# A recurrence of 512 steps on VectorE: copies, normaliser logarithms and output adds given to ScalarE and GpSimd, and the side work dealt over the eight steps anew

## The reference

```python
def step(state, inp):                       # state: (batch, head, 16, 16)
    r_t, k_t, v_t, w_t, a_t, kk_t = inp
    sa = jnp.einsum('bhij,bhj->bhi', state, -kk_t)
    state = w_t[..., None] * state + sa[..., None] * (kk_t * a_t)[:, :, None, :] + k_t[..., None] * v_t[:, :, None, :]
    norm = jnp.sqrt(jnp.mean(state * state, axis=-1, keepdims=True))
    state = state / (norm + EPS_STATE)
    o_t = jnp.sum(state * r_t[..., None], axis=-1)
    return (state, o_t)
...
out = g * out @ Wo.T
nrm = jnp.sqrt(jnp.mean(out * out, axis=-1, keepdims=True))
out = x_g + out / (nrm + EPS_RMS) * ln_weight      # x_g = x + 0.1 * convolution(x)
```

## Time and profile before

| | us |
|---|---|
| median of 3 runs (lowest, highest) | 2437.0 (2434.69, 2437.7) |
| the profiled execution's own time | 2441.28 |
| its span | 2439.2 |
| DVE busy | 2187.4 (90%) |
| PE busy | 1925.3 (79%) |
| ACT busy | 1585.6 (65%) |
| POOL busy | 903.2 (37%) |

### The profile page before, as it was taken

How to read it: one execution, slowest core, us unless ns; L and a number is a source line. 1 busy time by engine, 2 the same in 40 slices (tenths; PEclk the granted TensorE clock), 3 DMA queues, 4 the chain that set the end, 5 groups by cost and what they waited for, 6 DMA issues and landing times.

```text
span 2439.2 us, 47897 instructions
## 1 busy us (share of the span) xinstructions
PE 1925.3 (79%) x12321; PEld 1556.6 (64%) x12321; DVE 2187.4 (90%) x8800; ACT 1585.6 (65%) x5168; POOL 903.2 (37%) x1528
## 2 busy tenths in 40 slices
PE   5888888788888878888888878688887877344787
PEld 3555555455687867777777767677777767343555
DVE  6888887689619999999999999999999999999887
ACT  4878888577646665666666666666666565444776
POOL 0000000011105555555555555555555555555110
PEclk8999999699977787787877777987778777655899
DMA  5000000000000000000000000000000000000011
GB/s 183 17 17 22 17 21 23 3 1 1 1 1 1 1 1 1 1 1 1 1 1 1 1 1 1 1 1 1 1 1 1 1 1 1 1 1 1 1 35 35
DMA packets 14353, 25.02 MB, mean 10 GB/s; under 512 B 1280, under 2 KB 12032, under 8 KB 13824
## 3 DMA queue, kind: packets, MB, share of 16 engines
q1 hardware_dynamic: 14080, 21.97, 3.0%
HBM read 12.27 MB, written 4.19 MB: 7 GB/s over the span
## 4 chain that ended last, share of the span: by engine, by line
DVE 57%; issue 16%; PE 15%; ACT 6%; POOL 0%; DVEq 0%; POOLq 0%; ACTq 0%
DVE pn L1563 11%; DVE bank L1579 10%; DVE U L1620 8%; DVE xs L1551 5%; DVE bank L1568 5%; DVE kv L1612 4%; PE bank L282 3%; PE bank L267 2%; ACT prob L923 2%; PE bank L585 2%; DVE bank L1609 1%; PE bank L761 1%; DVE bank L1588 1%; DVE bank L1532 1%; PE bank L632 1%
## 5 line engine op out<-in xcount | busy, mean ns | idle before, releaser
L1748 POOL TENSOR_TENSOR wu<-U,stg 128x256 f32<-128x256 f32 x512 | 318.6, 622 | 682.2 <-DVE U L1620 682.2
L750 PE MATMUL bank<-U,ident 128*128 128x128 f32 x2048 | 464.2, 399 | 81.6 <-ACT go L1064 69.3
L750 PEld LDWEIGHTS bank<-U,ident 128*128 128x128 f32 x2048 | 426.7, 238 | 121.5 <-issue 90.6
L761 PE MATMUL bank<-stack,tm 128*128 128x64 f32 x1792 | 336.4, 374 | 145.7 <-ACT tm L994 137.2
L1213 ACT ACTIVATE xs<-U 128x128 f32<-128x128 f32 x1024 | 261.5, 302 | 275.5 <-DVE U L1620 271.6
L761 PEld LDWEIGHTS bank<-stack,tm 128*128 128x128 f32 x1792 | 325.6, 284 | 162.9 <-ACT tm L994 153.0
L1563 DVE TENSOR_REDUCE pn<-xs 128x16 f32<-128x256 f32 x1024 | 377.6, 408 | 0.6 <-issue 0.2
L1701 POOL TENSOR_TENSOR kv<-stg 128x256 f32<-128x256 f32 x513 | 318.7, 621 | 0.0
L1131 ACT ACTIVATE small<-pn 128x16 f32<-128x16 f32 x513 | 110.9, 216 | 295.0 <-DVE pn L1563 295.0
L735 PE MATMUL bank<-wcat,yT 128*128 128x224 f32 x1024 | 294.6, 447 | 2.5 <-issue 2.0
L1579 DVE TENSOR_TENSOR bank<-wu,bank 128x128 f32<-128x128 f32 x1024 | 292.0, 285 | 1.1 <-POOL wu L1748 0.8
(11 more groups left out here) (214 smaller groups left out, 3567.6 us busy)
## 6 DMA issues: line engine op xcount, KB each, us to landing
out_x<-x SPq DMA_DIRECT2D x8, 512.0 KB, 2.9
x<-in_x SPq DMA_DIRECT2D x1, 3584.0 KB, 17.7
Vs<-V SPq DMA_DIRECT2D x8, 384.0 KB, 4.6
...
```

The source lines that it names most:

```text
L750: last = pe.matmul(rsum.rearrange("p (t i) -> p t i", i=HD), ident[:, :], steps[:, :, :, j], start=(j == 0), stop=(j == HD - 1))
L761: last = pe.matmul(bank[3 + g][:, e * CH:(e + 1) * CH], tm[:, g * (PB // 2) + e, :, :].rearrange("p a c -> p (a c)"), stack[:, :], start=T ...
L1748: pool.tensor_tensor(ij(wu[:, :]), ij(U[:, half if j else 1 - half, (j - 1) % STEPS, :]), col(stg[:, half, j, TW, :]), ALU.mult).then_inc( ...
```

## The change

From DVE it takes the copies of kk and kk*a, the copies to `hist`, L1506, L1523 and L1528.

- The rows kk and kk*a are copied into bank 0 by ACT, in two operations for each half round (`copy_kk`, `copy_kka`), behind the squares of j = 2 and 6, and of j = 1 and 5. kk is taken from R directly; the slot for it in `stg`, and `stage_kk`, are gone. kk*a has two buffers, kk has one.
- ACT takes the logarithm straight from `sring`, twice a round (behind the squares of j = 0 and j = 4), 64 values each; `hist` is gone.
- These three wait for both L1551 of the next step (`beside_sums`), so that they run while DVE sums.
- A tile of the convolution, and of the output with its scale, is copied by ACT to `otmp` (`evacuate_convolution` in j = 5, `scale_outputs` in j = 7, both ahead of the squares). POOL multiplies the output by the weight and adds both to x.
- ACT's other side work moves: `evacuate_outputs` from behind the squares of j = 7 to ahead of those of j = 0, `factors` from j = 2 to ahead of those of j = 3, the second exponential of the decay and the small functions of the output's norm to ahead of those of j = 5, the gates' logarithm from j = 4 to j = 7.
- DVE waits for the copies of kk and kk*a at the first step of each half round, and once in each of jj = 1, 2 and 3, for the logarithm, for kk*a and for kk, before L1568.

The core of the diff (its waits on PE, which follow the new counts, and its semaphores' names are left out):

```diff
         zz = bank[0][:, 0:HD * HD]
-        kkz = bank[0][:, 256:384].rearrange("p (t q j) -> p t q j", q=2, j=HD)
-        sring = bank[0][:, 384:448].rearrange("p (t i) -> p t i", i=HD)
+        kkr = bank[0][:, 256:320].rearrange("p (t j) -> p t j", j=HD)
+        kkar = bank[0][:, 320:448].rearrange("p (g t j) -> p g t j", g=2, j=HD)
+        sring = bank[0][:, 448:512].rearrange("p (t i) -> p t i", i=HD)
...
+                act.activation(otmp, bank[6][:, 0:D], ACT.Copy).then_inc(C["x1"], 1)
...
+                act.activation(otmp, bank[6][:, 0:D], ACT.Copy, scale=oss[:, 2, 0:1]).then_inc(O["t"], 1)
+
+            def copy_kk(row):
+
+                act.activation(kkr, R[:, bass.ds(row, RENORM), QKK * HD:(QKK + 1) * HD], ACT.Copy).then_inc(S["kk"], 1)
+
+            def copy_kka(half, g):
+
+                act.activation(kkar[:, g, :, :], stg[:, half, g * RENORM:(g + 1) * RENORM, TKKA, :],
+                               ACT.Copy).then_inc(S["ka"], 1)
...
-                act.wait_ge(S["h"], last)
-                act.wait_ge(G["f2"], k)
-                act.activation(ls[:, :, :], hist[:, half, :, :], ACT.Ln).then_inc(G["ls"], 1)
+            def log_norms(g):
+
+                act.activation(ls[:, g * RENORM:(g + 1) * RENORM, :], sring, ACT.Ln).then_inc(G["ls"], 1)
+
+            def beside_sums(t1):
+
+                for e in range(2):
+                    act.wait_ge(T[e]["x"], t1)
...
                             if j == 0:
+                                if m >= 1:
+                                    evacuate_outputs(n, m - 1)
+                                elif n >= 1:
+                                    evacuate_outputs(n - 1, NB - 1)
                                 normalise(n, m)
...
                             if j == 3:
+                                factors(it, 1 - half)
                                 evacuate_features(n, m)
...
                             if j == 5:
+                                retention(1, it + 1, row_next)
                                 output_rms(n, m, 0)
+                                output_rms(n, m, 1)
+                                evacuate_convolution(n, m)
...
                             if j == 7:
                                 evacuate_pairs(n, m, 1)
+                                scale_outputs(n, m)
                             for e in range(2):
-                                act.wait_ge(T[e]["u"], t0 + (j + 1))
+                                act.wait_ge(T[e]["u"], t1)
                                 act.activation(xs[:, e, 1, :], rows8(U[:, half, j, :], e), ACT.Square).then_inc(T[e]["sq"], 1)
...
-                            if j == 7:
-                                evacuate_outputs(n, m)
+                            if t1 < L and (j + 1) % RENORM == 1:
+                                beside_sums(t1 + 1)
+                                act.wait_ge(S["sg"], t1)
+                                act.wait_ge(G["f2"], it + (j + 1) // RENORM)
+                                log_norms(0 if j + 1 > RENORM else 1)
+                            if t1 < L and (j + 1) % RENORM == 2:
+                                beside_sums(t1 + 1)
+                                if t1 > RENORM:
+                                    for e in range(2):
+                                        act.wait_ge(T[e]["z"], t1 - 2)
+                                act.wait_ge(G["ka"], it + 1 + g)
+                                copy_kka(half if g == 0 else 1 - half, 1 - g)
+                            if t1 < L and (j + 1) % RENORM == 3:
+                                beside_sums(t1 + 1)
+                                copy_kk(row_it + RENORM if g == 0 else row_next)
...
                             if jj == 0:
                                 dve.wait_ge(S["kk"], it * 2 + (g + 1))
+                                dve.wait_ge(S["ka"], it * 2 + (g + 1))
...
-                            if jj == 1:
-
-                                dve.wait_ge(S["sg"], t0 + j)
-                                if g == 0:
-                                    dve.tensor_copy(hist[:, 1 - half, RENORM:, :], sring).then_inc(S["h"], 1)
-                                else:
-                                    dve.tensor_copy(hist[:, half, 0:RENORM, :], sring).then_inc(S["h"], 1)
...
+                            if jj == 1:
+                                dve.wait_ge(G["ls"], it * 2 + (g + 1))
+                            if jj == 2:
+                                dve.wait_ge(S["ka"], it * 2 + (g + 2))
+                            if jj == 3:
+                                dve.wait_ge(S["kk"], it * 2 + (g + 2))
...
                             if j == 6:
-                                add_convolution(n, m)
                                 add_output(n, m, 0)
-                            if j == 7:
-                                add_output(n, m, 2)
...
                                 dve.reciprocal(lam, sring[:, jj - 1, :]).then_inc(S["lam"], 1)
-                                if g == 0:
-                                    kk_rows(half, 1)
-                                else:
-                                    dve.wait_ge(G["kk"], it + 2)
-                                    dve.wait_ge(G["ka"], it + 2)
-                                    kk_rows(1 - half, 0)
-                                if j == 7:
-                                    add_output(n, m, 3)
                                 dve.wait_ge(S["lam"], it * 2 + (g + 1))
...
+            def add_convolution(n, m):
...
+                pool.tensor_tensor(xt, xt, otmp, ALU.add).then_inc(C["x1"], 1)
...
+                pool.tensor_tensor(otmp, otmp, ln_w[:, :], ALU.mult).then_inc(O["t"], 1)
...
+                pool.tensor_tensor(xt, xt, otmp, ALU.add).then_inc(O["x"], 1)
```

158 lines of the change are left out of this document (86 added, 72 removed).

## The result

| | before | after |
|---|---|---|
| median of the runs, us | 2436.3 (2434.69 to 2437.7) | **2401.98** (2399.8 to 2405.28) |
| runs | 4 | 4 |
| ratio, with its 95% interval | 1 | 0.9861 (0.9843 to 0.9878) |
| profiled execution, us (span) | 2441.28 (2439.2) | 2399.92 (2398.1) |
| start of the recurrence, first to last product, rest | 724.95, 1528.6, 185.7 | 717.28, 1495.9, 184.9 |

The change makes the kernel faster by 34.3 us (1.4%); 2396.3 was predicted, within 2385 to 2412. The recurrence (from the first to the last L1572, in before L1551) is 32.7 us shorter. The other 8.4 of the profiled difference lie ahead of it (7.7) and behind it (0.7). In the twelve profiled executions of this study, whose code ahead of the recurrence is nearly the same, it starts anywhere from 713.3 us to 725.0 us, so I give that part no cause.

The account below looks back on a forecast made before the run. The recurrence was taken as bound by DVE, which was full while ACT was not. The terms 15.4 + 8.0 + 12.1 + 9.0 - 3.8 = 40.7 came off 2437.0, giving 2396.3 us, with an 8-in-10 range of 2385 to 2412.

Parts of the forecast that it names:

- output, 24 rounds: Step 7 of chunks 3, 5 and 7: removing L1523 and L1528 from DVE saves 0.64 each round, 15.4 us.
- convolution, 32 rounds: Step 6 in 32 rounds: removing L1506 from DVE saves 0.25 each, 8.0 us, as it partly covers a wait.
- `hist` copies: Steps 1 and 5: removing two copies a round saves 12.1 of 17.9 us, the rest covering waits for ACT's squares.
- kk copies: Rescaling steps: removing the copy saves 0.07, not 0.18, as L1609 waits for the reciprocal; 128 times, 9.0 us.
- more waits: First product of each half round: a third semaphore costs 0.03, 128 times, -3.8 us; ends 0 and -5.1.
- ACT late: Steps 0 and 5: ACT's operations ahead of the squares just fit, taken as 0; bound -10.8 us.
- POOL: POOL's 80 added operations fit its idle time, at most one a step: 0, unless `wu` is late.
- Rival 1: Steps 0 and 5: ACT's operations ahead of the squares don't fit; costs 10.8, giving 2407.1, or 2418 at twice that; chance 0.20.
- Rival 2: Step 5's wait for squares goes too, up to 5.8 more, and waits cost nothing, 3.8 more: 2387; chance 0.09.
- Rival 3: ACT's operations behind the squares delay the root by 0.1 in 384 steps: 38 us back, 2435; chance 0.04.
- Rival 4: DVE is held while POOL runs the 80 rounds' `otmp` adds and products: 49.6 us, 2445.9, slower; chance 0.05.
- Rival 5: DVE waits at the new semaphores as long as the removed operations took: 2413.6 at best, 2437 at worst; chance 0.03.

Follow-up runs that it names:

- experiment 2: Changed kernel without the two repeated copy waits at each half round's first product, row-sum wait moved to step 0's second multiplication: 2399.34 us, ratio 0.9838.
- experiment 3: Changed kernel with the `hist` copies back on DVE and ACT's logarithm reading `hist` again: 2413.72 us, one run.
- experiment 4: Changed kernel with the 64-value kk copy back on DVE between reciprocal and rescaling, kk*a staying on ACT: 2406.19 us, one run.
- experiment 1: Changed kernel with ACT's evacuation of the row sums moved from ahead of step 4's squares to behind them: 2397.86 us, ratio 0.9830.
- experiment 7: Changed kernel with the edits of experiment 1 and experiment 2, and wait orders swapped for root, sums and new state: 2350.57 us, ratio 0.9644.
- experiment 9: Changed kernel with `evacuate_outputs` back behind step 7's squares, now behind the gates' logarithm: 2399.33 us, one run.
- experiment 8: Changed kernel with two more 128x256 POOL operations per round, results unused: 2399.95 us, one run.

## Why the prediction came out as it did

**The recurrence** was to be shorter by 36 to 46 us, or the forecast was wrong by its own words. It is shorter by 32.7, or 36.0 by the medians of the steps, and the rest of the program moved as well, by 8.4 in the profiled executions. The time lies in the range, 5.7 us above the forecast; the sum was too high, and the range was wide enough. By terms:

| term | predicted | measured |
|---|---|---|
| output, 24 rounds | 15.4 | 15.4 (24 x (0.664 - 0.024)) |
| convolution, 32 rounds | 8.0 | 7.8 |
| `hist` copies | 12.1 | 10.8 (8.3 in step 1, 2.5 in step 5) |
| kk copies | 9.0 | 5.4 |
| more waits | -3.8 | -3.6 |
| ACT late | 0 (bound -10.8) | -0.5 (step 1 of chunks 2 and 4) |
| POOL | 0 | 0 |
| late squares of step 2 gone | not foreseen | 1.5 (24 x 0.064) |
| steps beyond their medians | not foreseen | -3.4 |

For kk and the waits the table of steps gives only their difference. Steps 3 and 7 won 0.027 and 0.024, times 64 (3.3), and steps 0 and 4 lost 1.5, which leaves 1.8. With the 3.6 of the waits (experiment 2) the copies come to 5.4. The late squares of step 2 are the 0.12 of experiment 3. The last term is what the medians don't hold; the column adds to 33.4, where 32.7 is the length measured, since the last step of all lies outside it.

**The term that was mis-sized** is that of the copies of kk: "So L1609 can come to 1130.42 from 1130.49: 0.07, not 0.18", times 128, 9.0. Its first half held: L1616 starts 0.29 behind the reciprocal, where 0.28 was forecast, and experiment 4 shows that this wait and not the copy sets it. What failed is that the 0.07 was carried to the end of the step unseen. Behind L1616's start the next product follows after 1362.40 - 1361.57 = 0.83 now, and after 1131.28 - 1130.49 = 0.79 in the earlier trace rows. Of these 0.04 the waits of the product are 0.016. The rest lies in L1616 itself: its two halves start 0.208 apart in the records instead of 0.192, and its mean is longer. The group in before and in after:

```profile
L1609 DVE TENSOR_TENSOR bank<-bank,small 128x128 f32<-128x128 f32 x254 | 60.8, 284 | 0.0
```

```profile
L1616 DVE TENSOR_TENSOR bank<-bank,small 128x128 f32<-128x128 f32 x256 | 63.7, 294 | 4.4
```

Why it is 10 ns longer is not shown. A copy of 64 values ahead of it (experiment 4) leaves its halves 0.208 apart too.

**The `hist` copies** went nearly as forecast step by step: 0.13 in step 1 (0.14), 0.036 in step 5 (0.05), nothing in chunks 1 and 6, all in chunk 7. The wait for the squares in step 5 was read rightly, and experiments 1 and 3 show it from both sides. Its size, 0.41 from the square's start to the sums, is 0.31 of squaring and 0.10 of hand-over, of which 0.06 was the order of the sums' own two waits (experiment 7). In chunk 1 the sums still come late, as in the earlier trace rows: 968.54 - 967.93 = 0.61.

```profile
967.93 0.47 DVE L1572 TENSOR_TENSOR xs<-U,bank 128x128 f32<-128x128 f32 x2
968.54 0.74 DVE L1577 TENSOR_REDUCE pn<-xs 128x16 f32<-128x256 f32 x2
```

**Rival 1** (ACT late in more steps) happened in the smallest form: step 1 of chunks 2 and 4 has its sums 0.412 behind the product and takes 2.830, 16 x 0.028 = 0.5 us. The margin of 0.1 that I had worked out from neighbours held in all other places and failed in these two. It was smaller than the 0.12 by which an evacuation can start later (see the last section).

**Rival 2** (more is won) didn't, but its parts were there to be had: the wait in step 5 gives 5.6 by the order of ACT (experiment 1), and the waits of the product 3.6 (experiment 2).

**Rival 3** (the root late) didn't, but experiment 9 shows it where one operation on ACT stands 0.12 later. What failed beside it is the premise that "this stretch is DVE's, and only what shortens DVE's chain shortens it". What I had missed is that the root was late all along, by the order of its own two waits. I had read the earlier trace rows (293.9 us idle, released by DVE) as ACT waiting for DVE, which is so, and concluded that DVE sets the pace, which isn't: 0.06 of each step was the hand-over itself. The forecast survived it because it went by differences between steps, not by busy time: output, `hist` and kk were ahead of the sums or behind the normaliser, where the same chain of DVE and ACT runs through DVE, and L1506, which stood beside the root, was counted with the 0.25 that it cost.

**Rival 4** (POOL takes what DVE gives) is excluded: the sums above leave nothing for it, and experiment 8 adds 78.8 us of POOL's work to no effect (sum of medians 1483.5 against 1483.8). That DVE's operands include one from a PSUM bank was among its counter-arguments. It is so for every two-input operation of DVE in the recurrence of after; in before one had not, other than was said ahead of the prediction and in this rival: L1528, `x<-x,y`, in 24 rounds, and POOL ran nothing beside those. Whether it matters isn't shown: no run changes where DVE's operands lie. What is shown is that POOL took longer for the convolution's add. L1738 takes 728 ns where DVE's L1506 took 410, and I had counted 0.62; that changes nothing, with 596.5 us of idle time:

```profile
L1778 POOL TENSOR_TENSOR wu<-U,stg 128x256 f32<-128x256 f32 x512 | 318.1, 621 | 596.5 <-DVE U L1627 596.5
L1738 POOL TENSOR_TENSOR x<-x,y 128x256 f32<-128x256 f32 x32 | 23.3, 728 | 0.0
```

**Rival 5** (DVE waits at the new semaphores as long as the copies took) didn't happen either: a half round pays 0.028 for its new waits (experiment 2).

**The multiplication that went to ACT** (L1099, 443 ns long there) cost the path nothing: taking the output's multiplication and add from DVE gave back the whole 15.4, as the rows said.

**DVE's busy time** fell by 2187.4 - 2143.1 = 44.3 us on the page. The operations taken away add to 95.5 (34.6 + 26.9 + 13.1 + 20.9), not to the 87 that the prediction gives; as it expected, the rest had overlapped with neighbours. Its "0.29 more" for ACT in steps 3 and 7 is 0.28 by its own numbers; nothing hangs on it.
